# Keys and values by plain fp32 products in chunks, a third of them ahead of the feed-forward part

## What is computed

```
x = x + L0_xattn(layernorm(x), ctx)   # a decayed sum over ctx, through W_in and W_out: one row per batch
x = x + L0_ffn(layernorm(x))          # rms norm, rows quantized to 8 bits, ternary weights w1 (2048x512) and w2 (512x2048)
x = x + L1_xattn(layernorm(x), ctx)   # 16 heads; q, out: int8 products
    k = cond @ wk.T + bk              # cond = ctx, fp32
    v = cond @ wv.T + bv
x = x + L1_ffn(layernorm(x))          # 8 experts, the best 2 per row
weight_quant(w): scale = 1 / max(mean(abs(w)), 1e-5); clip(round(w * scale), -1, 1) / scale
activation_quant(x): scale = 127 / max(max(abs(x)), 1e-5) per row; round and clip
```

## Time and profile before

| | us |
|---|---|
| median of 3 runs | 682.29 (682.21 to 684.25) |
| the profiled execution | 683.44 |
| its span, first to last instruction | 681.6 |
| TensorE busy in the span | 526.3 (77%) |
| VectorE, ScalarE, POOL busy | 374.9, 296.7, 197.7 |
| mean granted clock of TensorE | 0.911 of full speed |

### The profile page before, as it was taken

The page is one execution under the profiler, slowest core; times in us unless marked ns, Lnnn a source line. Parts: engine busy times, 40 slices in busy tenths (PEclk is TensorE's granted clock), DMA queues, the critical chain, the costliest instruction groups (busy, mean ns, idle before and its releaser), DMA issues.

```text
span 681.6 us, 11157 instructions
## 1 busy us (share of the span) xinstructions
PE 526.3 (77%) x3566; PEld 372.6 (55%) x3566; DVE 374.9 (55%) x1002; ACT 296.7 (44%) x631; POOL 197.7 (29%) x237
## 2 busy tenths in 40 slices
PE   0061549999999999977998989997751499999981
PEld 0040537777777777734776666775640255555540
DVE  4809738658658658547677776777445122222210
ACT  4147623443443443316997876786510022222220
POOL 1000123223223223133445545452524012222221
PEclk9997769999999999997998987998955599999996
DMA  8966333033033040040242231241342244554435
GB/s 326 421 229 247 124 124 124 0 123 123 0 123 123 0 139 1 0 165 1 82 164 57 95 108 52 71 136 56 105 117 68 80 76 83 93 91 81 83 44 127
DMA packets 32616, 72.64 MB, mean 107 GB/s; under 512 B 4002, under 2 KB 19394, under 8 KB 30522
## 3 DMA queue, kind: packets, MB, share of 16 engines
q1 hardware_dynamic: 28158, 63.48, 27.8%
q0 software_dynamic: 4416, 8.63, 7.9%
HBM read 46.40 MB, written 27.33 MB: 108 GB/s over the span
## 4 chain that ended last, share of the span: by engine, by line
PE 52%; DVE 20%; issue 8%; DMA 8%; POOL 5%; ACT 3%; SPq 1%; DVEq 0%; POOLq 0%; ACTq 0%
PE ps L1034 8%; PE ps L1020 7%; PE ps L773 7%; PE ps L760 7%; PE ps L863 4%; PE ps L793 4%; DMA y<-in_b_out 3%; PE ps L966 3%; PE ps L876 2%; PE ps L855 2%; DVE cxL L1105 2%; DVE sN L1342 2%; DVE VS L1086 1%; ACT hTe L707 1%; DMA VS<-in_wv 1%
## 5 line engine op out<-in xcount | busy, mean ns | idle before, releaser
L654 ACT ACTIVATE pE<-sN,nmx 100x361 f32<-100x361 f32 x128 | 77.8, 608 | 6.8 <-DVE nmx L1342 6.7
L1342 DVE CUSTOM_DVE_ANT_0 sN<-ps,maskS 100x361 f32<-100x361 f32 x128 | 62.0, 531 | 11.7 <-PE ps L855 6.1
L863 PE MATMUL ps<-ident,pE 100*121 100x100 f32 x384 | 61.9, 290 | 1.4 <-ACT pT L645 1.1
L552 POOL DMA_INDIRECT sums_out<-yb,backI x20 | 31.1, 1555 | 110.0 <-ACT yb L717 105.9
L863 PEld LDWEIGHTS ps<-ident,pE 100*121 100x121 f32 x384 | 50.8, 196 | 21.2 <-issue 19.9
L645 ACT COPY pT<-ps 121x300 f32<-121x300 f32 x128 | 52.0, 406 | 21.6 <-PE ps L863 21.3
L1034 PE MATMUL ps<-VS,hTe 118*128 x120 | 56.7, 609 | 5.5 <-ACT hTe L707 5.5
L1467 DVE TENSOR_TENSOR hb<-ps,b1B 128x352 f32<-128x352 f32 x20 | 10.5, 525 | 88.5 <-PE ps L1020 88.5
L1020 PE MATMUL ps<-CT,xT 128*128 x160 | 53.2, 476 | 2.0 <-DVE xT L1453 2.0
L1020 PEld LDWEIGHTS ps<-CT,xT 128*128 128x128 f32 x160 | 31.3, 197 | 24.9 <-issue 12.8
L1167 DVE TENSOR_REDUCE tk<-h 100x1 f32<-100x512 f32 x32 | 20.0, 679 | 39.7 <-ACT h L602 39.7
(11 more groups left out here) (252 smaller groups left out, 1183.1 us busy)
## 6 DMA issues: line engine op xcount, KB each, us to landing
slots_in<-zeros SPq DMA_DIRECT2D x8, 1848.0 KB, 8.0
VS<-in_w SPq DMA_DIRECT2D x8, 1024.0 KB, 8.6
CT<-in_ctxT SPq DMA_DIRECT2D x8, 728.0 KB, 17.1
CT<-in_ew SPq DMA_DIRECT2D x8, 704.0 KB
...
```

The costliest lines, as they stand in the source:

```text
L552: g.indirect_dma_start(sums_out, bass.IndirectOffsetOnAxis(backI[:, t:t + 1], 0), yb[:, t % 2, :], None, bounds_check=B * S + P - 1, compu ...
L654: act.activation(pE[0:S, q, 0:T], sN[0:S, q, 0:T], ACT.Exp, scale=-1.0, bias=nmx[0:S, h_:h_ + 1], accum_out=sums[0:S, j, h_:h_ + 1]).then_ ...
L863: mm = pe.transpose(ps[0:TC, 4 + r, c * S:(c + 1) * S], pE[0:S, h_ % HPC, c * TC:(c + 1) * TC], ident[0:S, 0:S])
L1342: dve.tensor_tensor_reduce(out=sN[0:S, q, 0:T], in0=ps[0:S, q, 0:T], in1=maskS[0:S, j, 0:T], scale=-1.0, scalar=3.4e38, op0=ALU.add, op1=A ...
```

## The change

- `wk` and `wv` are loaded into tensors of their own and used as they are, and so is the context: a chunk is four plain fp32 products, with no casts and no low parts.
- The context of batch b lies in the place of batch b + 1 in `CT` (the last in `ctx_last`), and the keys of batch b still go into `CT[:, b]`, which held the context ahead of it.
- The 56 chunks of all batches are numbered through, four of keys and three of values in turn (`q = 7 b + i`). Chunks 0 to 16 come ahead of the feed-forward part, between the summary's products and the weights' sums, over four banks; chunk 17 behind the first turn of the rows. From then on each batch takes the next five: two behind the first matrix (`early`), one behind the turned hidden rows (`mid`), one behind the second matrix (`late`), one behind the turned rows of the next batch (`last_`); the last batch takes the three that are left, all behind its first matrix. Banks 0 and 1 take turns there.
- Loads: all contexts and x come right behind `wk` and `wv`, then W_in and W_out, all of `w1`, and two quarters of `w2` into a tensor of their own (`ahead`).
- The loops are written out, with no hardware loop. `rows(b)` is done one batch further ahead than before.

```diff
-        wkH, wkL = sb(a, "wkH", [P, KC, D], F32R), sb(a, "wkL", [P, KC, D], F32R)
-        wvH, wvL = sb(a, "wvH", [P, KC, D], F32R), sb(a, "wvL", [P, KC, D], F32R)
-        cxH, cxL = sb(a, "cxH", [P, KC, TP], F32R), sb(a, "cxL", [P, KC, TP], F32R)
+        wkS, wvS = sb(a, "wkS", [P, KC, D]), sb(a, "wvS", [P, KC, D])
+        ctx_last = sb(a, "ctx_last", [P, KC * TP])
+        ahead = sb(a, "ahead", [P, 2, WP])
...
+        def ctx(b):
+
+            return CT[:, b + 1, :] if b < B - 1 else ctx_last[:]
...
+        def stage(w, c):
+
+            if w and c < 2:
+                return ahead[:, c]
+            at = 2 * NT * VW + (c - 2 * w) * WP
             return VS[:, at:at + WP]
...
-        def passes(eng, body):
-
-            with eng.Fori(0, B - 1) as b:
-                body(b, False)
-            body(B - 1, True)
+        KV = KC + NT
+        EARLY = 17
+
+        def bank_of(q):
+            return q % 4 if q < EARLY else q % 2
...
+        def beside(b):
+
+            at = EARLY + 1 + 5 * b
+            if b == B - 1:
+                return range(at, B * KV), (), (), ()
+            return range(at, at + 2), (at + 2,), (at + 3,), (at + 4,)
...
             sp.dma_start(biases[:, 0, :], b_in).then_inc(sem("biases_in"), 16)
             sp.dma_start(biases[:, 1, :], bk).then_inc(sem("biases_in"), 16)
...
+            sp.dma_start(ctx(0), ctxT[0]).then_inc(sem("ctx_in0"), 16)
...
+                sp.dma_start(ctx(b), ctxT[b]).then_inc(sem(f"ctx_in{b}"), 16)
+            sp.dma_start(XR[0:S], x).then_inc(sem(f"ctx_in{B - 1}"), 16)
+            sp.dma_start(w1s[:], win).then_inc(sem("win_in"), 16)
+            sp.dma_start(w2s[:], wout).then_inc(sem("wout_in"), 16)
+            for c in range(NW):
+                sp.dma_start(stage(0, c), w1[c]).then_inc(sem(f"stage_in{c}"), 16)
...
-            sp.dma_start(boutB, b_out.partition_broadcast(B)).then_inc(sem("win_in"), 16)
-            sp.dma_start(XR[0:S], x).then_inc(sem("vec_in"), 16)
+                sp.dma_start(stage(1, c), w2[c]).then_inc(sem(f"ahead_in{c}"), 16)
...
-            for c in range(NW):
-                sp.wait_ge(sem("ternary"), c + 1)
-                sp.dma_start(stage(2 + c), w2[c]).then_inc(sem(f"stage_in{(2 + c) % NW}"), 16)
...
+            for c in range(2, NW):
+                sp.wait_ge(sem("ternary"), c - 1)
+                sp.dma_start(stage(1, c), w2[c]).then_inc(sem(f"stage_in{c - 2}"), 16)
...
+            g.wait_ge(sem("vec_in"), 48)
+            g.wait_ge(sem(f"ctx_in{B - 1}"), 32)
+            norm_rows(0)
+            norm_ffn(0)
+            norm_rows(1)
+            for b in range(B):
+                half_rows(b)
+                if b < B - 1:
+                    norm_ffn(b + 1)
+                if b < B - 2:
+                    norm_rows(b + 2)
...
+                b, m = divmod(q, KV)
+                alone(act, ("k_mm", b * KC + m + 1))
+                act.activation(CT[:, b, m * TP:(m + 1) * TP], ps[:, bank_of(q), 0:TP], ACT.Identity,
+                               bias=biases[:, 1, m:m + 1]).then_inc(sem("k_copied"), 1)
...
+            for q in range(KC):
+                copy_keys(q)
+            for c in range(NW):
+                weight_sum(0, c)
+                copy_keys(KV + c)
+            act.wait_ge(sem("w_scale"), 1)
+            for c in range(NW):
+                round_chunk(0, c)
+            for c in range(NW):
+                if c:
+                    copy_keys(2 * KV + c - 1)
+                weight_sum(1, c)
+            act.wait_ge(sem("w_scale"), 2)
+            for c in range(2):
+                round_chunk(1, c)
...
+            rows_turned(0)
+            copy_keys(EARLY)
+            for c in range(2, NW):
+                round_chunk(1, c)
+            for b in range(B):
+                early, mid, late, last_ = beside(b)
...
+                take(early)
...
+                take(mid)
+                take(late)
+                if b < B - 1:
+                    rows_turned(b + 1)
+                take(last_)
...
+            def keys(b, m, at):
+                for k in range(KC):
+                    mm = pe.matmul(ps[:, at, 0:TP], wkS[:, k, m * P:(m + 1) * P], ctx(b)[:, k * TP:(k + 1) * TP],
+                                   start=(k == 0), stop=(k == KC - 1))
+                mm.then_inc(sem("k_mm"), 1)
+
+            def values(b, c, at):
+                for k in range(KC):
+                    mm = pe.matmul(ps[0:TC, at, :], ctx(b)[:, k * TP + c * TC:k * TP + (c + 1) * TC], wvS[:, k, :],
+                                   start=(k == 0), stop=(k == KC - 1))
+                mm.then_inc(sem("v_mm"), 1)
...
+            def chunk(q):
+
+                b, i = divmod(q, KV)
+                if not i:
+                    context_in(pe, b)
+                bank_freed(pe, bank_of(q), q)
+                if i < KC:
+                    keys(b, i, bank_of(q))
+                else:
+                    values(b, i - KC, bank_of(q))
+
+            for q in range(KC):
+                chunk(q)
+            pe.wait_ge(sem("ctx_in1"), 32)
+            for q in range(KC, KV):
+                chunk(q)
...
-            weight_total(0)
+            chunk(KV)
...
-            weight_total(1)
+            for q in range(KV + 1, KV + KC):
+                chunk(q)
+            weight_total(0)
+            for q in range(KV + KC, EARLY):
+                chunk(q)
...
-                for wt, cx in ((wkH, cxH), (wkL, cxH), (wkH, cxL)):
-                    for k in range(KC):
-                        mm = pe.matmul(ps[:, m % 2, 0:TP], wt[:, k, m * P:(m + 1) * P], cx[:, k, :],
-                                       start=(n == 0), stop=(n == 3 * KC - 1))
-                        n += 1
-                mm.then_inc(sem("k_mm"), 1)
...
-                keys(b, KC - 1)
+
+            turn_rows_in(0)
+            chunk(EARLY)
+            weight_total(1)
+            for b in range(B):
+                early, mid, late, last_ = beside(b)
...
-                values(b, 0)
-                values(b, 1)
+                for q in early:
+                    chunk(q)
...
-                values(b, 2)
+                for q in mid:
+                    chunk(q)
...
-
-            passes(pe, body)
+                for q in late:
+                    chunk(q)
+                if b < B - 1:
+                    turn_rows_in(b + 1)
+                for q in last_:
+                    chunk(q)
...
-            for i, (hi, lo) in enumerate(((wkH, wkL), (wvH, wvL))):
-                dve.wait_ge(sem("wkvH"), i + 1)
-                dve.tensor_tensor(lo[:].rearrange("p k n -> p (k n)"), stage(i),
...
+            def summary_sums(b):
+                context_in(dve, b)
...
-                for c in range(NT):
-                    if c == NT - 1 and not last:
-                        rows(b + 1)
-                    dve.wait_ge(sem("v_mm"), after(b * NT + c + 1))
-                    dve.tensor_copy(vs(b)[0:TC, c * VW:(c + 1) * VW], ps[0:TC, c % 2, :]).then_inc(sem("v_copied"), 1)
-                if not last:
-                    low_context(b + 1)
+                take(early)
                 ch(dve.tensor_scalar(tk[0:S, 22:23], tk[0:S, 19:20], wsc[0:S, 1, 1:2], 1.0 / QMAX, ALU.mult, ALU.mult))
-                if not last:
-                    ffn_rows(b + 1)
+                if b < B - 1:
+                    ffn_rows(b + 1, mid)
+                else:
+                    take(mid)
...
+                take(late)
+                if b < B - 2:
+                    rows(b + 2)
+                if b < B - 1:
+                    first_scale(b + 1)
+                take(last_)
+
+            dve.wait_ge(sem("vec_in"), 48)
+            dve.wait_ge(sem("rs_all"), 1)
             rows(0)
-            ffn_rows(0)
-            passes(dve, body)
+            w_scale(0)
+            ternary(0, 0)
+            copy_values(KV + KC)
+            ternary(0, 1)
+            copy_values(KV + KC + 1)
+            ternary(0, 2)
+            ternary(0, 3)
+            copy_values(KV + KC + 2)
+            ffn_rows(0, ())
+            w_scale(1)
+            for c in range(NW):
+                ternary(1, c)
+            first_scale(0)
+            rows(1)
+            for b in range(B):
+                body(b)
```

220 lines of the change are left out of this document (97 added, 123 removed).

## The result

The changed kernel takes 679.36 us (median of 20 runs, 676.67 to 684.04), against 684.0 for the kernel before in runs beside it: a ratio of 0.9939, 95% interval 0.9917 to 0.996. It is faster, but by 4.6 us (0.6%) where 21 were forecast, and 679.36 lies above the range of 648 to 673. The profiled execution took 677.46 us (span 675.5), 6.0 less than that of before.

What follows compares the result with a forecast made beforehand. It took TensorE's work to bound the loop and everything else the front; loop -16.8, front -3.3 and tail -1.0 sum to -21.1 us, from the median 682.29 to 661.1, range 648 to 673.

Steps and rivals of the forecast that it cites:

- The products: Keys and values chunks: eight instructions each, keys 2.45 us (+0.45), values 3.42 us (+0.66).
- rival 2: Keys and values chunks: a plain product as long as four fp32r products, loop +8.0 us, 669 in all; chance 0.07.
- The loop: First to last turn of hidden rows: 162.5 us against 179.3, a gain of 16.8.
- The tail: Last turn of hidden rows to end of last residual add: 7.0 us against 8.03, a gain of 1.0.
- The front: Up to the first turn of hidden rows: at 104.7 us against 108.02, a gain of 3.3.
- seven contexts and x, 6.7 MB, 16 us: they are in at 28: Front, loads behind the values' weights: all landed at 28 us, the sums over them soon after.
- output sums 8 x 0.43, to 46.2: Front, behind chunk 7 (to 42.7): eight output-sum instructions of 0.43 us, ending at 46.2.
- an estimate of 2 us for the way back, behind the last loads: 51.4: Front, summary row: 1.8 us out and 2 us back, there at 51.4, before row work of 4.1.
- The clock: TensorE's low level after pauses: 1.8 us charged per start; input sums 6.96 us, thought to run ahead of it.
- rival 1: Warm front: its pauses and input sums do not cost the low level, 5 to 6 us less, 655; chance 0.15.
- Rival 4: Front never reaches TensorE's upper level: its 18 chunks cost 99.8 us, slower by 20, 702 in all; chance 0.05.
- Rival 5: Front: little change, half of the cold-front rival as weights stall behind chunks, 682 in all; chance 0.03.

Runs made afterwards that it cites:

- thin chunks: The changed kernel with one product in place of four in chunks 7 to 17: 670.75 us, ratio to before 0.9855.

## Why the prediction was wrong

By its own steps:

- *The products*: right. A plain product is two instructions, those of values 0.43 us apart, those of keys near 0.305. That is 0.61 us a product of keys against the 0.165 of one of fp32r, 3.7 times and not quite the four of rival 2. The Trainium skill's four passes ("FP8 and Floating Point Precision", "TensorE Precision Notes") give the direction, and a size that is 8% too high here.
- *The loop*, 162.5: measured 162.76. The 14 table loads are gone, one start at the low level is left (charged 1.8; the first turn takes 1.2 in place of 0.7 and the chunk of values behind it 4.07 in place of 3.42, by the starts of the weight loads), the waits are there (3.4 forecast in all, 3.4 for hidden rows alone). The price was not forecast but follows from its terms: 20 x 0.45 + 16 x 0.66 = 19.6 on paper, 12.7 in the run. A cheaper chunk uncovers the wait for hidden rows, 8.0 us in six batches in place of 3.4; the other 2.3 are not accounted for.
- *The tail*, 7.0: measured 6.73.
- *The front*, 104.7: measured 120.79. This is the step that failed, in its terms for transfers: two of them set the result, and a third lay hidden behind these.
  1. "seven contexts and x, 6.7 MB, 16 us: they are in at 28". They are in at 36.66, since everything moves at half rate while x does, and W_in behind x at 39; so the input sums start 7.4 us late.
  2. "output sums 8 x 0.43, to 46.2", right behind chunk 7. They wait for `wout_in`, which counts the load of `b_out` as well, and that was issued behind six quarters of weights: 57.84. The page of before had said it: its first product of all was released by `b_out` at 40.27. I used the row for its 6.96 us and did not read its bracket; the run of before with this load early shows that it cost 4.6 us there already.
  3. "an estimate of 2 us for the way back, behind the last loads: 51.4". In the changed kernel itself this held, 4.3 us from the end of the add to the row work against 4.1, since `b_out` had made the row wait for the queue to empty. With `b_out` early and x late the last loads are still on the way until near 60, and a row issued behind them takes 10.7 us out in place of 1.8. This term then takes the place of the second, and so the first two did not add up.
- With the loads in the order of need the same work gives 108.3: 12.5 of the 16.1 us are shown to come from how the loads were issued (with x in parts and its statistics moved). The remaining 3.6 are, by the timeline, the quarters of `w1` that wait for the queue (scale of w1 at 60.1, forecast 55.9); no run shows them gone.
- *The clock*: the input sums were to take 6.96 us as they "ran in front of the low level". They take 4.47 and 3.63 us where they follow chunk 6 without a pause (x late with `b_out` early, and the row on GpSimd's queue), so 6.96 is their time at the low level. In those runs this gives back 2.5 to 3.3 us of what rival 1 had in mind; in the changed kernel they waited for W_in and took 6.96.
- *Rival 4*, a cold front, did not come: between its pauses TensorE reaches the upper level. *Rival 5*, at 682, came nearest to the measured 679.36, but its cause, weights stalled behind chunks, moved the first turn by 2.6 us only in the run with thin chunks.

The range was made of uncertainties in engine work, "a front some 6 us off". No case let a transfer set the front.
